# Down product of the 64-row half: high and low rows side by side in 128 stationary columns

## What is computed

```
sel, w   = top 8 of 48 kept experts per token, weights normalised      (4096 tokens)
xb[e]    = the first 192 tokens routed to expert e                      (192 x 512)
g, u     = split(xb[e] @ gate_up[e].T)                                  (192 x 192 each)
h        = silu(g) * u                                                  (192 x 192)
y[e]     = h @ down[e].T                                                (192 x 512)
out      = x + sum over e of w * y[e], added to the rows of its tokens
```

## Time and profile before

| | value |
|---|---|
| timed runs, median (lowest to highest) | 1068.07 us (1064.69 to 1069.98) |
| profiled execution, own time | 1064.81 us |
| its span, first to last instruction | 1063.1 us |
| mean granted TensorE clock | 0.986 of full speed |
| busy: PE / weight loads / DVE / ACT / POOL | 96% / 79% / 79% / 59% / 53% |

### The profile page before, as it was taken

The page is one execution under the profiler, slowest core; times in us unless marked ns, Lnnn a source line. Parts: engine busy times, 40 slices in busy tenths (PEclk is TensorE's granted clock), DMA queues, the critical chain, the costliest instruction groups (busy, mean ns, idle before and its releaser), DMA issues.

```text
span 1063.1 us, 24370 instructions
## 1 busy us (share of the span) xinstructions
PE 1016.1 (96%) x6564; PEld 835.6 (79%) x6564; DVE 835.3 (79%) x2255; ACT 624.7 (59%) x1751; POOL 560.9 (53%) x565
## 2 busy tenths in 40 slices
PE   5999799999999999999999997899999999999994
PEld 4787687887887887887877875688888888888883
DVE  5777587887887887888888876378888888888883
ACT  4555455555545545545555553177777777777772
POOL 3225466566567666666666666623443434434334
PEclk9999899999999999999999999799999999999998
DMA  7999584453331221211311514168999999999995
GB/s 274 376 306 254 209 292 183 145 213 138 101 116 50 77 72 50 87 61 50 98 50 50 210 40 159 41 207 236 255 261 248 263 251 256 262 241 263 252 224 69
DMA packets 90644, 185.75 MB, mean 175 GB/s; under 512 B 23943, under 2 KB 24071, under 8 KB 89712
## 3 DMA queue, kind: packets, MB, share of 16 engines
q1 hardware_dynamic: 59232, 145.13, 42.6%
q0 software_dynamic: 31376, 40.20, 16.8%
HBM read 116.04 MB, written 122.00 MB: 224 GB/s over the span
## 4 chain that ended last, share of the span: by engine, by line
PE 54%; issue 13%; POOL 13%; DMA 9%; DVE 8%; ACT 1%; SPq 1%; DVEq 1%; POOLq 0%; ACTq 0%
PE ps L1236 15%; PE ps L1392 14%; PE ps L1426 9%; POOL slot_records L594 7%; PE ps L1221 5%; DMA arena<-in_x 4%; PE ps L1408 3%; PE ps L1226 3%; POOL rstd L605 2%; DVE qk_both L1058 2%; DMA arena<-slot_records 2%; DMA layer_out<-qk_both,slot_table 2%; POOL arena L650 1%; PE ps L1334 1%; PE ps L1263 1%
## 5 line engine op out<-in xcount | busy, mean ns | idle before, releaser
L594 POOL DMA_INDIRECT slot_records<-row,slot_idx x240 | 243.3, 1014 | 80.2 <-issue 50.8
L679 POOL DMA_INDIRECT layer_out<-qk_both,slot_table x96 | 145.1, 1511 | 218.2 <-DMA layer_out<-qk_both,slot_table 190.7
L605 POOL TENSOR_TENSOR rstd<-mv,neg_half 128x1 f32<-128x1 f32 x96 | 67.8, 706 | 125.5 <-DVE mv L976 78.6
L1236 PE MATMUL ps<-w_high,xn_high 128*128 128x512 f32 x384 | 114.1, 419 | 0.7 <-ACT xn_high L700 0.7
L735 ACT ACTIVATE arena<-ps,neg_max 128x128 f32<-128x128 f32 x256 | 89.9, 377 | 31.9 <-DVE neg_max L968 31.9
L1236 PE MATMUL ps<-w_high,xn_low 128*128 128x512 f32 x384 | 107.3, 401 | 0.0
L1236 PE MATMUL ps<-w_low,xn_high 128*128 128x512 f32 x384 | 107.2, 401 | 0.0
L700 ACT ACTIVATE xn_t<-ps 128x512 f32<-128x512 f32 x64 | 38.3, 599 | 100.8 <-PE ps L1221 100.7
L1392 PE MATMUL ps<-w_high,w_low 128*128 128x192 f32 x576 | 87.8, 274 | 0.0
L1392 PE MATMUL ps<-w_low,w_high 128*128 128x192 f32 x576 | 87.7, 274 | 0.0
L1392 PE MATMUL ps<-w_high 128*128 128x192 f32 x576 | 86.8, 272 | 0.4 <-DVE w_low L1143 0.4
(11 more groups left out here) (164 smaller groups left out, 2468.5 us busy)
## 6 DMA issues: line engine op xcount, KB each, us to landing
gu_sb<-in_gate_up SPq DMA_DIRECT2D x48, 768.0 KB, 5.4
slot_records<-arena SPq DMA_DIRECT2D x6, 3366.0 KB, 25.1
arena<-slot_records SPq DMA_DIRECT2D x48, 280.5 KB, 4.8
dn_sb<-in_down_proj SPq DMA_DIRECT2D x48, 256.0 KB, 5.4
arena<-in_x SPq DMA_DIRECT2D x32, 256.0 KB, 2.7
x_res<-in_x SPq DMA_DIRECT2D x32, 256.0 KB, 3.0
ctx_t_sb<-in_ctx_t SPq DMA_DIRECT2D x32, 256.0 KB, 3.5
ctx_sb<-in_ctx_rows SPq DMA_DIRECT2D x32, 256.0 KB, 4.0
```

The costliest lines, as they stand in the source:

```text
L594: pool.indirect_dma_start(out=records, out_offset=bass.IndirectOffsetOnAxis(ap=slot_idx_of(s)[:, k:k + 1], axis=0), in_=row_of(s), in_offs ...
L605: pool.tensor_tensor(rstd[:, :], mv[:, 1:2], neg_half[:, 0:1], ALU.pow).then_inc(steps.sem, 1)
L679: pool.indirect_dma_start(out=out, out_offset=bass.IndirectOffsetOnAxis(ap=slot_table[0:PART[h], 2 * d.index + h:2 * d.index + h + 1], axi ...
L1236: last = pe.matmul(dst, left[:, c, :], right[:, m, c, :], start=(n == 0 and c == 0), stop=(n == 2 and c == KC - 1))
```

## The change

The second half of the tokens (64 rows) is computed with three products in place of five. The high and low columns of h stand side by side in one buffer (`h1_parts`, `h2_parts`, 384 columns: 192 high, then 64 low of the second half, then 128 low of the first half), so that `MIXED` (columns 128 to 255) is 64 high and 64 low columns. One product of these 128 columns with `dn_high` gives high x high in PSUM rows 0 to 63 and low x high in rows 64 to 127; high x `dn_low` goes to rows 0 to 63; one product of the mixed `h2` columns with `dn2_both` gives the rest. The two row halves are added at the eviction: ScalarE copies rows 64 to 127, times the weight, into `y`; VectorE then computes rows 0 to 63 times the weight plus that copy. For this the 64 weights of the second half are also put on partitions 64 to 127. The low parts of h are made in two instructions each, since their columns are no longer in order. The first half keeps its five products.

```diff
-                                  (P, 2, 1, CAP), (P, 2, 1, CAP)):
+                                  (P, 2, 1, 2 * CAP)):
...
+        LEFT = (slice(2 * CAP - P, 2 * CAP), slice(CAP, 2 * CAP - P))
+        MIXED = slice(P, 2 * CAP - P)
...
-        def h2_low(e):
-            return h2_rest[HALVES[e.parity], e.parity, 0, :]
+        def h1_low(e, h):
+            return h1_parts[:, e.parity, 0, LEFT[h]]
+
+        def h2_low(e, h):
+            return h2_parts[HALVES[e.parity], e.parity, 0, LEFT[h]]
...
-        dwn_a = Steps(sem("down_scalar"), "y0")
+        dwn_a = Steps(sem("down_scalar"), "y0 y1_rest")
...
+                    act.wait_ge(dwn_t.sem, dwn_t.after(d, "y1"))
+                    copy(y[PART[1]:P, d.parity, 1, :], ps[PART[1]:P, 5, :], dwn_a,
+                         scale=weight_of[d.parity][PART[1]:P, 1:2])
...
-                    left_by(h1_low[:, u.parity, 0, :], h1[:, :], h1_high[:, u.parity, 0, :]).then_inc(gup_v.sem, 1)
+                    for h in range(2):
+                        left_by(h1_low(u, h), h1[:, part(h)], h1_high[:, u.parity, 0, part(h)]).then_inc(gup_v.sem, 1)
...
-                    left_by(h2_low(u), h2[:, :], h2_high[:, u.parity, 0, :]).then_inc(gup_v.sem, 1)
+                    for h in range(2):
+                        left_by(h2_low(u, h), h2[:, part(h)], h2_high[:, u.parity, 0, part(h)]).then_inc(gup_v.sem, 1)
                 if d.exists():
+                    dve.wait_ge(dwn_a.sem, dwn_a.after(d, "y1_rest"))
                     dve.wait_ge(dwn_t.sem, dwn_t.after(d, "y1"))
...
-                    dve.tensor_scalar(y[0:PART[1], d.parity, 1, :], ps[0:PART[1], 5, :],
-                                      weight_of[d.parity][0:PART[1], 1:2], None, ALU.mult).then_inc(dwn_v.sem, 1)
+                    dve.scalar_tensor_tensor(y[0:PART[1], d.parity, 1, :], ps[0:PART[1], 5, :],
+                                             weight_of[d.parity][0:PART[1], 1:2], y[PART[1]:P, d.parity, 1, :],
+                                             ALU.mult, ALU.add).then_inc(dwn_v.sem, 1)
...
-                    dve.tensor_copy(weight_of[t.parity][:, :],
-                                    rows[:, t.parity, :, bass.ds(t.index + DM, 1)]
-                                    .rearrange("p h o -> p (h o)")).then_inc(ffn_w.sem, 1)
+                    for dst, h, size in ((slice(0, P), 0, P), (slice(0, PART[1]), 1, PART[1]),
+                                      (slice(PART[1], P), 1, PART[1])):
+                        dve.tensor_copy(weight_of[t.parity][dst, h:h + 1],
+                                        rows[0:size, t.parity, h, bass.ds(t.index + DM, 1)]).then_inc(ffn_w.sem, 1)
...
-                        pairs = [(h1_high, dn_high, P), (h1_high, dn_low, P), (h1_low, dn_high, P),
-                                 (h2_twice, dn2_both, P), (h2_rest, dn2_both, P)]
...
+                        else:
+                            steps = [(P, h1_parts[:, e, 0, MIXED], dn_high),
+                                     (PART[1], h1_parts[:, e, 0, P:CAP], dn_low),
+                                     (P, h2_parts[:, e, 0, MIXED], dn2_both)]
+                        for i, (n, left, right) in enumerate(steps):
+                            last = pe.matmul(ps[0:n, 4 + h, :], left, right[:, e, 0, :],
+                                             start=(i == 0), stop=(i == len(steps) - 1))
```

More of the change, by code:

```diff
@@ L249, in split_buffers @@
                 at += size
-        gu_high, rows_high, dn_high, dn2_both, h1_high, h2_twice = split_buffers(w_high)
-        gu_low, rows_low, dn_low, _, h1_low, h2_rest = split_buffers(w_low)
+        gu_high, rows_high, dn_high, dn2_both, h1_parts = split_buffers(w_high)
+        gu_low, rows_low, dn_low, _, h2_parts = split_buffers(w_low)
+        LEFT = (slice(2 * CAP - P, 2 * CAP), slice(CAP, 2 * CAP - P))
+        MIXED = slice(P, 2 * CAP - P)
         HALVES = (slice(0, INTER - P), slice(INTER - P, P))
-        h2_high, h2_again = h2_twice[HALVES[0]], h2_twice[HALVES[1]]
+        h1_high = h1_parts[:, :, :, 0:CAP]
+        h2_high, h2_again = h2_parts[HALVES[0], :, :, 0:CAP], h2_parts[HALVES[1], :, :, 0:CAP]
         def dn2_raw(e):
@@ L345, in decoder_layer @@
         gup_a = Steps(sem("gate_up_scalar"), "silu1 silu2 high1 high2 again")
-        gup_v = Steps(sem("gate_up_vector"), "h1 h2 low1 low2")
+        gup_v = Steps(sem("gate_up_vector"), "h1 h2 low1_0 low1 low2_0 low2")
         wgu_a = Steps(sem("gate_up_weights_scalar"), "high")
@@ L353, in decoder_layer @@
         ffn_v = Steps(sem("rows_vector"), "low0 low1")
-        ffn_w = Steps(sem("rows_vector_kept"), "tokens weight")
+        ffn_w = Steps(sem("rows_vector_kept"), "tokens weight0 weight1 weight")
         dwn_t = Steps(sem("down_tensor"), "y0 y1")
         dwn_v = Steps(sem("down_vector"), "y1")
-        dwn_a = Steps(sem("down_scalar"), "y0")
+        dwn_a = Steps(sem("down_scalar"), "y0 y1_rest")
         def raw(m):
@@ L1172, in expert_turn @@
                         for parity in range(2):
-                            dve.memset(h2_rest[HALVES[1 - parity], parity, 0, :].bitcast(FP32), 0.0)
-                    left_by(h2_low(u), h2[:, :], h2_high[:, u.parity, 0, :]).then_inc(gup_v.sem, 1)
+                            dve.memset(h2_parts[HALVES[1 - parity], parity, 0, CAP:2 * CAP].bitcast(FP32), 0.0)
+                    for h in range(2):
+                        left_by(h2_low(u, h), h2[:, part(h)], h2_high[:, u.parity, 0, part(h)]).then_inc(gup_v.sem, 1)
                 if d.exists():
+                    dve.wait_ge(dwn_a.sem, dwn_a.after(d, "y1_rest"))
                     dve.wait_ge(dwn_t.sem, dwn_t.after(d, "y1"))
@@ L1421, in expert_turn @@
                                 pe.wait_ge(dwn_v.sem, dwn_v.after(d.back(1), "y1"))
-                        dst = ps[0:PART[h], 4 + h, :]
-                        pairs = [(h1_high, dn_high, P), (h1_high, dn_low, P), (h1_low, dn_high, P),
-                                 (h2_twice, dn2_both, P), (h2_rest, dn2_both, P)]
-                        for i, (left, right, n) in enumerate(pairs):
-                            last = pe.matmul(dst, left[0:n, d.parity, 0, part(h)], right[0:n, d.parity, 0, :],
-                                             start=(i == 0), stop=(i == len(pairs) - 1))
+                        e = d.parity
+                        if h == 0:
+                            steps = [(P, h1_parts[:, e, 0, 0:P], dn_high), (P, h1_parts[:, e, 0, 0:P], dn_low),
+                                     (P, h1_parts[:, e, 0, LEFT[0]], dn_high), (P, h2_parts[:, e, 0, 0:P], dn2_both),
+                                     (P, h2_parts[:, e, 0, LEFT[0]], dn2_both)]
+                        else:
[5 more added lines that the diff above has]
+                                             start=(i == 0), stop=(i == len(steps) - 1))
                         last.then_inc(dwn_t.sem, 1)
```

## The result

The changed kernel takes 1100.75 us, median of six runs (1099.98 to 1112.63). Six runs of the kernel before give 1067.12 us (1063.59 to 1069.98). The ratio is 1.0335, with a 95% interval of 1.0287 to 1.0382: slower by 33.6 us. The forecast had the sign and the place, but 14 us where 33.6 came, and its range ended at 1098.

The account below looks back on a forecast made before the run. TensorE was taken as the bound, VectorE's loop close behind: 7.06 - 0.46 + 0.81 + 0.01 + 0.40 = 7.82 us a turn against 7.34. Then 1064.81 + 20.2 - 3.7 = 1081.3, stated as 1082 us, range 1068 to 1098.

Parts of the forecast that it names:

- VectorE's loop: Chain from down product through VectorE's eviction and weight parts to the next: 7.06 us a turn, forecast to become 7.82.
- The low parts of h in four instructions: VectorE's two extra instructions: forecast to cost nothing, hidden in its wait before the eviction; without cover up to 0.61 us.
- The three weight copies: Three copies for one in VectorE's loop: forecast +0.40 us a turn, with bounds of nothing and 0.62.
- A switch between partition halves: Rival: three switches in VectorE's loop lose overlap, 0.36 us a turn, giving 1097 us; chance 0.18.
- The clock: Rival: TensorE's granted clock falls because it stands waiting; ten such turns would give 1140 us; chance 0.05.
- TensorE's lead over it is only 0.27 us: Per turn, TensorE's 7.33 us against VectorE's loop of 7.06, so TensorE was taken as the bound.
- a hand-over of 0.05 us: From the end of VectorE's "low2" to TensorE going on; counted in the 7.06 us of VectorE's loop.
- The copy's price, 0.81 us: ScalarE's copy 0.69 plus hand-over to VectorE 0.12, ahead of VectorE's eviction, in its loop; bounds 0.69 and 1.12.
- the 0.46 saved: Two matmuls fewer at 0.23 us each: the 64-row half ends 0.46 us earlier for TensorE and VectorE's loop.
- It stays just beside the loop: ScalarE's high part of the gate/up weights, 1.49 us, queued behind the copy, was claimed not to lengthen VectorE's loop.
- At 7.82 us a turn they keep up: Output adds, at 7.39 us a step, no longer fall behind until the last two turns; 3.7 us given back.
- the rival that the adds stay late: Rival: DMA queues still lag, the 3.7 us at the end aren't given back, 1085 us; chance 0.08.

Follow-up runs that it names:

- 3: Changed kernel, VectorE evicting rows 0 to 63 without waiting for or adding ScalarE's copy, which stays: 1093.85 us, ratio 1.0235.
- 4: Kernel before, its 64-row half with three of its five products, both with low parts of h left out: 1079.01 us, ratio 1.0074.
- 2: Changed kernel, with the wait for "low2" as the last of TensorE's waits ahead of the down product: 1092.62 us, ratio 1.0228.
- experiment 1: Kernel before, with only the three weight copies in place of one: 1074.66 us, ratio 1.0056.
- 7: Kernel before, with three weight copies and "low2" as TensorE's last wait: 1068.94 us, ratio 1.0022.
- 10: Kernel before, with only "low2" moved to be TensorE's last wait: 1068.52 us, ratio 1.0022.
- 6: Changed kernel, with "low2" as TensorE's last wait and ScalarE's copy as VectorE's last wait ahead of the eviction: 1084.68 us, ratio 1.0197.
- 9: Changed kernel without the addition, ScalarE's copy at the end of its turn and without its weight: 1066.97 us, ratio 1.0017.
- experiment 5: Changed kernel without the addition, ScalarE's copy, still weighted, at the end of its turn: 1192.75 us, ratio 1.1181.
- experiment 12: Changed kernel, both late waits last, weights in a table, token numbers, weight copies and gate/up split ahead of the evictions: 1127.14 us, ratio 1.0579.

## Why the prediction was right in sign and wrong in size

**Right.** The mechanism: VectorE's loop becomes the bound through ScalarE's copy, and TensorE stands ahead of the down product until "low2" is there. The low parts of h in four instructions are hidden: VectorE still waits 0.95 us behind them. (Without the wait for the copy they would not quite be: in 3 the eviction follows them without a pause, at 2.37 us, where it starts at 2.27 in 4.) The three weight copies came out at +0.33 us a turn against 0.40. A switch between partition halves that costs 0.36 us more on top is not seen: it would have given 0.76 there. Whether a smaller price of it is among the 0.33 was not tried apart. The clock stayed at 1.00.

**The step that failed: "TensorE's lead over it is only 0.27 us".** It rests on a hand-over of 0.05 us from a written-out turn, put into a loop whose turns are of another kind. There the way from "low2" to the weight load is 0.33 us where TensorE waits for "low2" alone, as in the changed kernel (2). With it VectorE's loop was 2.72 + 1.19 + 3.08 + 0.33 = 7.32 us long, not 7.06: nearly as long as the turn. The table's own 0.34 for the kernel before could not have shown this, since the four parts add up to the turn whatever bounds it; that the lead was only 0.05 us, experiment 1 shows. The hand-over was thus 0.28 us a turn too low in the sum, 42 x 0.28 = 11.8 us of the 35.8. Experiments 7 and 10 are the controls: with the hand-over shortened, the lead exists.

**The copy's price, 0.81 us, was 1.01** (+0.55 with the 0.46 saved). It lay within its bounds of 0.69 and 1.12. Half of the 0.20 is the hand-over, 0.24 us for 0.12, with waits behind the late one (6). The other half is the copy's start, 2.35 us after the weight load (median), where the prediction's terms give 2.72 - 0.46 = 2.26. The way from TensorE to ScalarE, taken to be 0.54 us, is 0.60 from the start of a half's last product (median, first half); 0.60 behind 836.65 is 837.25. And ScalarE is not quite free: it ends the first half's eviction and starts the copy about 0.03 us later still. Over 42 turns: +8 us. With the copies' 0.07 less, 0.28 + 0.20 - 0.07 = 0.41 us a turn accounts for the 8.19 - 7.82 = 0.37 by which the turn was missed, to within 0.04.

**"It stays just beside the loop"** was right, by 4.79 - 4.64 = 0.15 us, and its meaning was missed: ScalarE's list behind the copy is a limb almost as long as VectorE's. Without the addition the turn is still 8.03 us (3), and only with both limbs cleared does the loss go (9).

**"At 7.82 us a turn they keep up"** failed, and the rival that the adds stay late held. The last add starts 1090.81 - 1085.51 = 5.3 us behind the last eviction, where it was 6.4, and the end gave back 0.3 us, not 3.7. The 7.39 us a step of the earlier trace rows was not a fixed price of the adds: at 8.19 us a turn they keep about the same distance, and one takes 6.2 us from issue to landing (median over all adds) where it took 5.5. They did keep up in experiment 5, at 9.7 to 10.8 us a turn: there they start 1.5 us behind the eviction and land after 4.5 us. Why the landing takes longer in some kernels is open; no run measured it apart from the turn's loads.

**The gain that the change aimed at was not there to take.** Experiment 4 gives two products away and is not faster. Before the change, TensorE's list (10) and VectorE's loop (1) stood within 0.05 us of 7.33 us. The ScalarE limb was some 0.2 us shorter: it sets the turns of 4 that the adds leave alone (median 7.12). And the output adds hold up single turns already where the others take 7.0 to 7.4 us, in the profiled executions of 4, 7, 9 and 10, and most turns of 12. For the shorter executions of 4 no trace shows what holds them.

## What to carry to other kernels

Take the time of a hand-over from turns of the same kind as those that are summed, and put the wait that ends last at the end of an instruction's waits. Before cutting the busiest engine, measure each loop that closes over a turn, with every limb through another engine's list: where several are equally long, the cut gives nothing, and whatever is added to any of them is paid in every turn. A new wait has to be followed along two paths, the engine that waits and the list behind the instruction that it waits for: here either one alone cost nearly the whole price.

## What the runs showed of the hardware

- A wait that ends last costs more where others stand behind it in a looped turn: from VectorE's last write to TensorE's weight load 0.325 us with three behind it, 0.05 or 0.12 with none (2); from ScalarE to VectorE 0.24 and 0.14 (6). Whether it is the number of waits or the registers in them was not tried apart; the written-out turn with the same list took 0.05.
- The granted clock stayed 1.00 (2.4 GHz) in the changed kernel, where TensorE stands about 1.3 us ahead of a down product, and the matmul behind that wait took 0.49 us. In experiment 5 the clock was 0.84 over the stretch shown, a mixture of the two levels: TensorE stood 2.8 us in every other turn, and the matmul behind that took 0.79 us, while the one behind the 1.15 us of a turn between took 0.49. So waiting for others cost time on TensorE too.
- The output adds, at 7.39 us a step in the kernel before, followed the turn up to 8.19 us with a lag of 6 to 7 us; at 9.7 to 10.8 us a turn the lag was 1.5 (5). At turns of 7.0 to 7.4 us they could stop the evictions for 3 to 4 us (4, 7, 9, 10). The median from issue to landing was 5.5 us in the kernel before, 6.2 in the changed one, 6.9 in experiment 12 and 4.5 in experiment 5, at DMA shares of 0.97, 0.85, 0.79 and 0.76 from 800 to 900 us: a lower share did not always go with a faster landing. The cause is open.
